# A cross-interaction tower on one core: the 24 product arrays of a tile are halved twice by accumulating DMAs

## The reference

```python
def _cin_layer(X0, Xi, W, b):
    Wr = W.reshape(H, F0_, Fi)
    return jnp.einsum('hjk,bjd,bkd->bhd', Wr, X0, Xi) + b[None, :, None]
...
for W, b in Ws:                      # three layers, X0 is (512, 39, 16), H = 128
    Xi = _cin_layer(X0, Xi, W, b)
    res.append(Xi.sum(axis=2))       # 3 x 128 features of a sample
...
h = jnp.concatenate([z, dense_ctx], axis=1)      # (512, 400)
h = jnp.maximum(h @ W_top1 + b_top1, 0.0)        # 400 -> 512
h = jnp.maximum(h @ W_top2 + b_top2, 0.0)        # 512 -> 256
y = h @ W_top3                                   # 256 -> 1
```

## Time and profile before

| what | value |
|---|---|
| median of 3 runs | 673.1 us (672.78 to 676.59) |
| the profiled execution | 672.67 us |
| its span, first to last instruction | 670.6 us |
| busy PE, DVE, ACT, POOL | 641.9, 521.2, 488.3, 361.1 us |
| busy shares of the span | 96%, 78%, 73%, 54% |
| DMA queue 0 (issued by GpSimd), queue 1 (by SyncE) | 42.0% and 21.2% of the 16 engines' time |
| mean granted TensorE clock | 0.995 |

### The profile page before, as it was taken

How to read it: one execution, slowest core, us unless ns; L and a number is a source line. 1 busy time by engine, 2 the same in 40 slices (tenths; PEclk the granted TensorE clock), 3 DMA queues, 4 the chain that set the end, 5 groups by cost and what they waited for, 6 DMA issues and landing times.

```text
span 670.6 us, 11899 instructions
## 1 busy us (share of the span) xinstructions
PE 641.9 (96%) x2516; PEld 461.4 (69%) x2516; DVE 521.2 (78%) x1478; ACT 488.3 (73%) x1692; POOL 361.1 (54%) x308
## 2 busy tenths in 40 slices
PE   0689999999999999999999999999999999999998
PEld 0246777777777777777777777777777777785483
DVE  0346888878888888888888878888888888897590
ACT  1137877778787868787877878787868787897293
POOL 6878766575656565755666675656575221121000
PEclk9799999999999999999999999999999999999999
DMA  6457687767676777667667767676777657567100
GB/s 225 60 92 168 112 183 133 173 131 162 124 160 128 159 150 163 142 134 155 139 144 134 167 130 161 124 160 129 160 150 162 142 102 178 126 122 215 31 1 0
DMA packets 61944, 91.05 MB, mean 136 GB/s; under 512 B 34599, under 2 KB 38548, under 8 KB 61671
## 3 DMA queue, kind: packets, MB, share of 16 engines
q0 software_dynamic: 14192, 51.02, 42.0%
q1 hardware_dynamic: 47734, 39.85, 21.2%
HBM read 10.59 MB, written 1.28 MB: 18 GB/s over the span
## 4 chain that ended last, share of the span: by engine, by line
PE 91%; POOL 3%; DMA 3%; issue 2%; SPq 1%; ACT 0%; DVE 0%; ACTq 0%; POOLq 0%
PE t_bank L426 22%; PE t_bank L427 21%; PE t_bank L428 21%; PE x_bank L394 14%; PE small_bank L411 5%; POOL emb L324 3%; PE t_bank L491 1%; PE t_bank L471 1%; PE t_bank L502 1%; PE t_bank L503 1%; PE t_bank L514 1%; PE t_bank L505 1%; DMA emb<-in_table,idx 1%; PE x0t_bank L402 1%; DMA emb_scratch<-emb 1%
## 5 line engine op out<-in xcount | busy, mean ns | idle before, releaser
L567 ACT ACTIVATE prod<-t_bank,x0t 128x128 f32<-128x128 f32 x1472 | 417.5, 377 | 114.6 <-PE t_bank L428 109.3
L671 DVE SCALAR_TENSOR_TENSOR prod<-t_bank,x0t,prod 128x128 f32<-128x128 f32 x1024 | 287.9, 343 | 80.1 <-PE t_bank L428 75.8
L426 PE MATMUL t_bank<-w_hi,x_hi 128*128 128x512 f32 (+1 forms) x640 | 307.5, 480 | 0.6 <-DVE x_lo L660 0.3
L427 PE MATMUL t_bank<-w_lo,x_hi 128*128 128x512 f32 (+1 forms) x640 | 247.8, 387 | 0.0
L428 PE MATMUL t_bank<-w_hi,x_lo 128*128 128x512 f32 (+1 forms) x640 | 247.0, 386 | 0.0
L324 POOL DMA_INDIRECT emb<-in_table,idx x160 | 211.8, 1324 | 48.5 <-issue 46.8
L334 POOL TENSOR_TENSOR diag<-x0t,mask 128x320 f32<-128x320 f32 x64 | 87.8, 1372 | 195.4 <-DVE prod L671 97.7
L426 PEld LDWEIGHTS t_bank<-w_hi,x_hi 128*128 128x128 f32 x640 | 120.2, 188 | 54.7 <-issue 29.7
L427 PEld LDWEIGHTS t_bank<-w_lo,x_hi 128*128 128x128 f32 x640 | 120.5, 188 | 47.1 <-issue 25.3
L428 PEld LDWEIGHTS t_bank<-w_hi,x_lo 128*128 128x128 f32 x640 | 120.1, 188 | 24.2
L703 DVE TENSOR_TENSOR prod<-prod 128x768 f32<-128x768 f32 (+2 forms) x192 | 117.4, 611 | 6.0 <-DMA prod<-prod 5.7
(11 more groups left out here) (73 smaller groups left out, 242.8 us busy)
## 6 DMA issues: line engine op xcount, KB each, us to landing
prod<-prod POOLq DMA_DIRECT2D x63, 768.0 KB, 7.1
shared<-rep SPq DMA_DIRECT2D x96, 234.0 KB
shared<-rep SPq DMA_DIRECT2D x48, 78.0 KB
emb<-in_table,idx POOLq DMA_INDIRECT x160
G<-in_w SPq DMA_DIRECT2D x1, 2496.0 KB
rep<-rep SPq DMA_DIRECT2D x28, 78.0 KB
rep<-emb_scratch SPq DMA_DIRECT2D x20, 78.0 KB
prod<-in_w SPq DMA_DIRECT2D x1, 1536.0 KB, 7.1
```

The lines of the kernel that those rows point to most:

```text
L426: pe.matmul(acc, hi, w1_hi[:, cols], start=True, stop=False)
L427: pe.matmul(acc, hi, w1_lo[:, cols], start=False, stop=False)
L567: last = act.activation(prod[:, s, SLOT[c] + u, :], t_bank[c % T_BANKS][:, u * H:(u + 1) * H], ACT.Copy, scale=x0t[:, s, j:j + 1])
L671: last = dve.scalar_tensor_tensor(unit, t_bank[c % T_BANKS][:, u * H:(u + 1) * H], x0t[:, s, j:j + 1], unit, ALU.mult, ALU.add)
```

## The change

Arrays 0 to 5 and 6 to 11 that the first fold leaves are added by a second accumulating DMA (`fold_again`). GpSimd issues it at the end of its work for the tile two after, behind the second of two halves into which the diagonal is cut. VectorE has three steps left, of 3, 1 and 1 arrays, behind chunks 3, 5 and 7, three tiles behind. G comes behind chunk 0 of the tile four later. In the last tile VectorE adds the arrays of tiles 60 and 61, with the second halving of 61 on VectorE, and TensorE takes G of tile 60 at chunk 7. Behind it come first tile 63, folded twice by VectorE, and then tile 62. The dense part of the tower's first layer is spread over four strips of 16 rows at partitions 0, 32, 64 and 96, one for each PSUM bank, with eight small loads in place of two; one of four tower products with G's last feature moves behind the third layer's last product.

```diff
+QUARTER = HALF // 2
-LEFT = (HALF, 6, 3, 2)
-BEHIND = 2
+LEFT = (QUARTER, 3, 2)
+BEHIND = 3
-RED = 4
+RED = 3
+J_SPLIT = J1 // 2
-WT1_LOADS = 3
+STRIP = P // M1
+WT1_LOADS = 1 + 2 * M1
-G_AT = 2
+G_AT = 0
+LAST_G_AT = 7
+LAST_G_COPY_AT = 9
-SUM_AT = (1, 3, 5, 7)
+SUM_AT = (3, 5, 7)
+LAST_SUM_AT = {3: ((0, 0), (0, 1)), 5: ((0, 2), (1, 0)), 7: ((1, 1), (1, 2))}
...
+            for m in range(M1):
+                strip = slice(m * STRIP, m * STRIP + D)
+                cols = slice(m * P, (m + 1) * P)
+                sp.dma_start(wt1[strip, 3, cols], top1[3 * P:, cols]).then_inc(wt1_loaded, 16)
+                sp.dma_start(dense[strip, :], dense_t).then_inc(wt1_loaded, 16)
...
+            def diagonal(t, slot, part, first):
+                if part == 0:
+                    pool.wait_ge(x0t_ready, t + 1)
+                    if not first:
+                        pool.wait_ge(g_mm, t - TILES_PER_GROUP + 1)
+                js = slice(0, J_SPLIT) if part == 0 else slice(J_SPLIT, J1)
...
+            def fold_again(slot):
+                pool.dma_start(prod[:, slot, 0:QUARTER, :].rearrange("p j h -> p (j h)"),
+                               prod[:, slot, QUARTER:HALF, :].rearrange("p j h -> p (j h)"),
+                               accum_op=ALU.add).then_inc(refolded[slot], 16)
...
                     if fold_before:
                         scaled(t - 1)
-                    diagonal(t, s, first)
+                    diagonal(t, s, 0, first)
                     if fold_before:
                         fold((s - 1) % TILES_PER_GROUP)
...
+                    fold_twice = not (first and s < 2) and not (last and s == TILES_PER_GROUP - 1)
+                    if fold_twice:
+                        pool.wait_ge(folded[(s - 2) % TILES_PER_GROUP], (g + (1 if s >= 2 else 0)) * 16)
+                    diagonal(t, s, 1, first)
+                    if fold_twice:
+                        fold_again((s - 2) % TILES_PER_GROUP)
...
-                pe.wait_ge(diag_ready, t + 1)
+                pe.wait_ge(diag_ready, (t + 1) * 2)
...
+                        if last and s == TILES_PER_GROUP - 1 and c == LAST_G_AT:
+                            g_product(t - BEHIND, 0)
...
             for m in range(M1):
                 if m == 2:
+                    g_product(TILES - 3, 1)
                     pe.wait_ge(act_scaled, TILES * NA)
                     pe.wait_ge(dve_scaled, TILES * ND)
-                if m == M1 - 1:
-                    g_product(TILES - 2, 2)
-                first_layer(m, P, 0, z0[:, :], start=True)
-                first_layer(m, D, 3, dense[:, :])
-            g_product(TILES - 1, 3)
+                first_layer(m, 0, z0[:, :], start=True)
+            pe.wait_ge(diag_ready, TILES * 2)
+            g_product(TILES - 2, 3)
+            for m in range(M1):
+                strip = slice(m * STRIP, m * STRIP + D)
+                pe.matmul(h1_bank[m][:, :], wt1[strip, 3, m * P:(m + 1) * P], dense[strip, :],
+                          start=False, stop=False, tile_position=(m * STRIP, 0))
+            g_product(TILES - 1, 2)
...
-            for m in range(M1):
-                first_layer(m, P, 1, G[:, F, :])
+            for m in range(M1 - 1):
+                first_layer(m, 1, G[:, F, :])
...
+            first_layer(M1 - 1, 1, G[:, F, :])
             pe.wait_ge(z2_ready, 1)
...
+                for i, n in enumerate((HALF, QUARTER)):
+                    if i > 0:
+                        dve.wait_ge(last_folded, i)
+                    dve.tensor_tensor(prod[:, slot, 0:n, :], prod[:, slot, 0:n, :], prod[:, slot, n:2 * n, :],
+                                      ALU.add).then_inc(last_folded, 1)
...
-            for i in range(RED):
-                sum_over_j(TILES - 2, GROUPS - 1, 2, i)
             fold_last(TILES - 1, 3)
             for i in range(RED):
-                sum_over_j(TILES - 1, GROUPS - 1, 3, i, by_dve=True)
+                sum_over_j(TILES - 2, GROUPS - 1, 3, i, by_dve=True)
+            refold(2)
+            for i in range(RED):
+                sum_over_j(TILES - 1, GROUPS - 1, 2, i, by_dve=True)
```

More of the change, by code:

```diff
@@ L130, in tower_program @@
         wt1 = shared
-        dense = sb("dense", [D, B])
+        dense = sb("dense", [P, B])
         w3 = sb("w3", [P, M2])
@@ L358, in _, with group @@
                 gather(i, 0)
-            def group(g, half, first=False, gathers=True, early=True):
+            def group(g, half, first=False, gathers=True, early=True, last=False):
                 for s in range(TILES_PER_GROUP):
@@ L383, in _ @@
             group(GROUPS - AHEAD, 0, gathers=False, early=False)
-            group(GROUPS - 1, 1, gathers=False, early=False)
+            group(GROUPS - 1, 1, gathers=False, early=False, last=True)
         @block.tensor
```

54 lines of the change are left out of this document (31 added, 23 removed).

## The result

The changed kernel takes 708.8 us (median of 4 runs, 705.76 to 716.35) against 673.2 beside it: ratio 1.050, 95% interval 1.046 to 1.054. The forecast was 674.2 with a range up to 685, so it missed by far more than its range. Medians are of all executions of a kernel; the ratios and their intervals leave out those more than 1.5% above its shortest. The profiled execution took 706.07 us, with a span of 704.3 and a mean granted clock of 0.983 (before: 672.67, 670.6 and 0.995).

What follows compares the result with a forecast made beforehand. TensorE's own matmuls were taken to bound the groups. +2.8 us for G's place and -1.7 behind the last tile gave +1.1 on 672.67, so 673.8, or 674.2 with the median 0.4 higher; range 668.5 to 685.

Steps and rivals of the forecast that it cites:

- SyncE and the DMA share: SyncE's store, copy and factor-load chain 1 to 3 us longer, DMA share 0.70 to 0.92; price 0, ends 0 and 0.3 per group.
- next to nothing: From 100 to 560 us, VectorE's waits for anything but TensorE, which it waits 68.5 us for.
- G's new place: G behind chunk 0: TensorE about 0.2 us late for x2, once in each of 14 groups, +2.8 us.
- The far end of 0.5 per group: Upper bound of G's term, if VectorE's steps before x2 stretch: 7.0 us in all.
- The second halving: Lands at 335.5, 0.2 us before VectorE's first add in the tight tile; price 0, bounds 0 and 0.7 us per group.
- Rival 2: Second halving late in each group's first tile: 0.9 us per group, 12.6 in all, 684.0 us; chance 0.20.
- The figure of 2.9 us: Time for the GpSimd-issued second halving by the Trainium skill; the measured row of 5.7 at best was put ahead of it.
- GpSimd: GpSimd's queue has room for the added work: its sequence is 8.2 us of a tile's 9.0.
- Behind the last tile: Strips, reordered last tiles and the moved product behind the last tile: -1.7 us, between -2.5 and +1.5.
- Wrong altogether: Signs that would refute the forecast: TensorE waiting for t-bank releases or pair products, or a group below 35.9 us.
- the 0.23 for slower: Chance of over 1% slower, from Rival 2 and the upper end of 0.5 per group in G's term.

Runs made afterwards that it cites:

- experiment 5: Kernel before plus an accumulating DMA of 384 KB per tile into a spare array nobody reads; adds, G and tail as before: 708.9 us, 1.051.
- experiment 1: Changed kernel with the second halving back on VectorE as an add of six arrays, no second accumulating DMA: 681.8 us, 1.012.
- experiment 2: As experiment 1, with a group's first pair product behind the last add of x2 instead of in front of it: 673.7 us, 1.000.
- experiment 4: Changed kernel with G back behind chunk 2 instead of chunk 0: 726.3 us, 1.080.
- experiment 3: Changed kernel with a group's first pair product behind the last add of x2: 702.7 us, 1.040.
- experiment 9: Kernel before plus the unread 384 KB DMA per tile, with the next group's rows stored, loaded and copied early between factor loads: 696.0 us, 1.036.
- experiment 11: As experiment 10, with GpSimd issuing the second halving ahead of the first halving and the gathers: 761.1 us, 1.130.
- experiment 7: Changed kernel with SyncE storing, loading and copying the next group's rows between the current group's factor loads: 701.1 us, 1.034.
- experiment 10: Changed kernel with the next group's rows early between factor loads and the first pair product behind x2's last add: 688.1 us, 1.020.

## Why the prediction was wrong, step by step

**The failed step is "SyncE and the DMA share."** The prediction put the DMA share at 0.92 (measured 0.90; the second halvings took 59.4% of 704.3 less 42.0% of 670.6 us, by 61, or 2.2 us of the engines each, 2.0 forecast) and said that the chain "will be 1 to 3 us longer" (measured 3.6 at the median, 13.4 to 17.0). Then it took the price as 0, with 0.3 us per group as the far end, since "VectorE has its spare 1.0 us right there". Measured were 27.3 us over fourteen groups, 2.0 each, and the traffic alone makes 2.2 each (experiment 5). Two things were wrong in it. The cover was looked for in VectorE's spare time and not in SyncE's ring, whose store waits until this group's loads are out and whose slack of about 3.8 us the chain used up. And a delay of 1.66 to 4.93 us is no longer covered by 1.0 us of spare time. The wait of 1.3 us for the factors in the earlier trace rows was a sign that this place was already near the edge before, as was a first turn of the ring with a chain of 17.2 us. The wait was read as "next to nothing".

**G's new place** was right in kind and place. The second tile's x2 is 0.27 late where 0.23 was worked out, 0.3 with the repair as the measure. The low part's 0.1 was not foreseen; both are in experiments 1 and 2. The far end of 0.5 per group holds for both together. In the changed kernel the step matters more than its sum: it leaves VectorE's wait for the factors no room before TensorE stops, which the prediction didn't combine with its own 1 to 3 us.

**The second halving** was predicted to land 3.7 to 5 us after its issue and lands at 4.5/7.6/10.2 (shortest, median, longest), no faster than the full one at 5.8/7.3/10.1. Rival 2 named this, and its price was seen in part only: 5.2 us of waits in the stretch from 100 to 560 us, since the same late factors held the adds' tiles back anyway; 20.4 once the rows went early. The duration was built from engine time of 2.0 us plus a fixed 1.7, with 1 us for sharing; at a share of 0.90 the median lies 3.9 above the 3.7. The figure of 2.9 us by the Trainium skill (DMA: Bandwidth & Descriptors, "Anatomy of one DMA") is further off still. It describes one transfer, and here four kinds are under way.

**GpSimd** was costed at 0 by its queue's length of 8.2 us of 9.0. The sum holds, but the wait in front of it, for a G of the same tile, was overlooked. At chunk 0 it costs nothing that can be told apart here; at chunk 2 it costs 17.5 us (experiment 4).

**Behind the last tile** -1.7 was predicted and -2.24 came in the profiled execution, with the strips at once: 1.42 up to the second-layer products, where 0.8 was forecast, and 0.8 for the moved product, where it was 0.9. The sum had no term for the clock. The new order stops TensorE for 1.8 us in front of a G, and where the clock then falls to 0.50, as in experiments 1 and 2, the gain is gone (58.64 and 58.74 us against 58.29 before). The Trainium skill (TensorEngine Tiling (Array Packing), "Key Properties") says that different tiles can run in parallel, and with a bank each the four did. The same section speaks of a drain at the change of mode, and the rows leave little room for one: the first strip starts 654.87 - 654.16 = 0.71 us after its G. A product of z followed a G after 0.54 and 0.64 us before (612.31 to 612.85, 619.07 to 619.71), a chunk after 0.37 (345.80 to 346.17 in experiment 1). That would be 0.1 to 0.3 us, once.

**"Wrong altogether"** came near the sign that came true: TensorE waiting for pair products, directly in experiments 3 and 5, by way of x2 and G in the changed kernel. No rival stood for it and no chance was given to it: the 0.23 for slower was worked out from rival 2 and the upper end of G's term, and the range ended at 685.

What stays open: how much of the 16.6 us left in experiment 9 each transfer makes (first factors or later ones), why a late ring costs 2 us at once, and why the clock falls behind the same pause in one execution and not in another. The second layer's weights land later with the traffic, at 8.1 to 9.6 us from their issue against 6.8 to 7.1 before, but in experiment 5 this costs nothing behind the last tile.

## What to carry to other kernels

Before adding bytes to the DMA engines, write down every ring of dependent transfers that runs once per group, with its length and its slack against the group; here 3.8 us of slack was the whole margin, and a DMA share of 0.90 in place of 0.70 used it up. To price traffic before the real edit is made, issue the same transfer to an array that nobody reads: here it gave 708.9 us where the change took 708.8, without any of the new adds, if not by the same parts. And when an instruction moves earlier, look at what stands in front of its producer, since two small lacks of slack at one place add up to a stop of TensorE.

## What the runs showed that was not expected

- Half the bytes need not land sooner beside busy engines: 384 KB took 7.6 us at the median where 768 KB took 7.3, at a DMA share of 0.90. Issued ahead of the 768 KB (experiment 11), they took 5.0, and the 768 KB 9.5.
- The DMA share does not tell the landing. The same 768 KB took 7.1 us at a share of 0.70, 7.3 at 0.90, 8.2 at 0.91 (experiment 7), 7.1 at 0.93 (experiment 10) and 9.5 at 0.84 (experiment 11).
- The clock fell to the 1.2 GHz level during a pause of TensorE of 5 us (0.50 from 320 us on) and was still there 3 us after it had resumed. Behind the last tile a pause of 1.8 us was followed by the same fall in six kernels of eight, at a price of 2.6 us or more.
- Four matmuls of K = 16 on row strips, each to its own bank, start within 0.01 us of each other, and all eight instructions are done 1.1 us after the first start (654.87 to 656.01), where each one took 1.12 us before.
